# Grouped attention: a key's rotation, scalings and split spread over three heads

## The chip, the cores and the metric

The kernel runs on one core of a Trainium2 chip. The metric is the device time of one execution in microseconds (us), median of the runs. A core has engines that run side by side, each with its own instruction queue, and synchronise by semaphores: TensorE (PE, matrix products into PSUM; its weight loads are listed as PEld), VectorE (DVE), ScalarE (ACT), GpSimd (POOL) and SyncE (SP), which here issues the DMA transfers.

## The reference

A stack of two hybrid layers over x of shape (2, 512, 512), all in float32: narrow-head attention, two gated feed-forward blocks round a selective scan, grouped attention, a routed low-rank block, a top-k gated feed-forward block and the low-rank block again; each takes a layer-normalised x and is added to x. The change is in the grouped attention: 32 query heads of width 128 share 8 keys and values, four heads to a key.

```
q = q * cos + rotate_half(q) * sin          # the rotation, queries and keys
k = k * cos + rotate_half(k) * sin
scores = einsum('bhqd,bhkd->bhqk', q, k) / sqrt(128)
key_scale = where(kpos < 35, 0.5, where(kpos < 107, 1.5, 1.0))
scale = where(qpos >= 107, key_scale, 1)    # rows from 107 on only
probs = softmax(scores * scale + causal)
attn = einsum('bhqk,bhkd->bhqd', probs, v);  out = attn @ wo.T
```

## The kernel before, in words

The kernel writes each engine's program out by hand, in one order, with counted semaphores. A product of float32 matrices is made of three matmuls over operands that are split into a rounded high part and the difference as low part.

Grouped attention is the stage `gqa(b)`, run once for each batch b. Each engine has a function of that name; DVE's is at line 1542, PE's at 874, ACT's at 1179, and POOL's loop is at 573. All go through the heads h = 0 to 31 (GH = 32, G_REP = 4 heads to a key, G_KV = 8 keys). In the DVE and PE loops `part` is h % 4 and `g` is h // 4 - 1, the group of heads that has just been finished.

The work of a head is pipelined over several iterations. PE in iteration h makes the scores of head h + 1, turns the normalised probabilities of head h, projects the query of head h + 3 (into bank 7), makes the values product of head h, and in between one or two of the four output tiles of the group before: tiles 0 and 1 where part is 0, tile 2 where it is 1, tile 3 where it is 2. All four output tiles and the projected keys go through the one PSUM bank 3. PE waits there, by `claim(3, s["x_added"])`, until DVE has added the tile before into x. The next key but one is projected where part is 3.

A projected query or key becomes a rotated one as follows. DVE multiplies it by the cosines (`times_cos`, line 1546: `g_qc` for a query, `g_kc` for a key). ACT copies the two halves swapped into `g_sw` (two buffers, lines 1187 and 1188). POOL multiplies that by the sines (line 583), splits up to three weight units (lines 557 and 558), and for a query makes the low part (line 590), for which it needs the high part from DVE. DVE adds the two (`rope`, line 1551). For a query (`rope_q`) it then rounds the high part (line 1568). For a key (`rope_k`) it makes the high and low part of the first 128 columns (lines 1558, 1559), scales 35 columns by 0.5 and 72 by 1.5 (1560, 1561), and splits the whole key (1312, 1313 in the helper `split`); `g_k_split` tells PE that it may be used, which it does in the scores of head 4(g + 2), made in iteration 4(g + 2) - 1.

In DVE's iteration: the row maxima of the scores of head h + 1 (lines 1572 to 1602), a copy of a turned tile (1587), the low part of the values (1591), the rotation of the query of head h + 2, in heads 4, 8, ... 24 the rotation of a key, the cosine product of the query of head h + 3, two reciprocals of the row sums (1581), which ACT's normalising (line 1204) needs, and the adds into x (`add_rows`, line 1316).

Of the kernel before, what the change touches and what calls it, by code (L numbers as in the profile page):

```python
# [38 lines left out]
G_KV, G_REP, G_HD = 8, 4, 128  # L39
# [193 lines left out]
def hybrid_layers(nc, x_d, units_d, const_d, small_d, bdown_d, out_d):  # L233
# [9 lines left out]
    with ExitStack() as ctx:  # L243
# [3 lines left out]
        s = {n: ctx.enter_context(nc.semaphore(n)) for n in SEMS}  # L247
# [35 lines left out]
        def cut(stage, words, parts=1, dt=F32):  # L283

            at = cuts.get(stage, 0)
            cuts[stage] = at + words
            base, size = areas["rows" if stage in ("n", "l", "m_rows", "k_rows", "a_o") else "stages"]
            assert cuts[stage] <= size, (stage, cuts[stage])
            t = nc.alloc_sbuf_tensor_at(f"{stage}_{at}", [P, words * 4 // mybir.dt.size(dt)], dt, offset=base + 4 * at, align_bytes=4)
            return t[:, :] if parts == 1 else t[:, :].rearrange("p (a c) -> p a c", a=parts)  # L290
# [39 lines left out]
        g_sw, g_qk, g_kk = cut("g", 1024, 2), cut("g", 1024, 2), cut("g", 512)  # L330
# [3 lines left out]
        g_k_hi, g_k_lo = f_hi, f_lo  # L334
# [33 lines left out]
        def col(name, lo=0, hi=None):  # L368
            a, b = (CONST if name in CONST else SMALL)[name]
            t = const if name in CONST else small  # L370
            return t[:, a + lo:(a + hi if hi is not None else b)]
# [931 lines left out]
        def _(dve):  # L1303
# [6 lines left out]
            def split(hi, lo, src, sem):  # L1310

                did(V.tensor_copy(hi, src))
                did(V.tensor_tensor(lo, src, hi.bitcast(F32), ALU.subtract), sem)

            def add_rows(b, t, bank):
                go(V.tensor_tensor(x[:, b, t], x[:, b, t], ps[:, bank], ALU.add), s["x_added"])  # L1316
# [225 lines left out]
            def gqa(b):  # L1542
                dve.wait_ge(s["rope_in"], 16)
                def times_cos(out, bank, sem):
                    need(sem)
                    did(V.tensor_tensor(out, ps[:, bank], col("cos"), ALU.mult), s["g_cos"])

                def rope(out, part):

                    need(s["g_rot"])  # L1550
                    did(V.tensor_tensor(out, part, g_sw[:, done["swap"] % 2], ALU.add), s["g_roped"])  # L1551
                    done["swap"] += 1

                def rope_k(g):
                    rope(g_kk, g_kc)

                    k0, g = g_kk[:, 0:P], g % 2
                    did(V.tensor_copy(g_k0_hi[:, g], k0))  # L1558
                    did(V.tensor_tensor(g_k0_lo[:, g], k0, g_k0_hi[:, g].bitcast(F32), ALU.subtract))
                    go(V.tensor_scalar(g_kk[:, 0:SYS], g_kk[:, 0:SYS], 0.5, None, ALU.mult))  # L1560
                    did(V.tensor_scalar(g_kk[:, SYS:IMG], g_kk[:, SYS:IMG], 1.5, None, ALU.mult))
                    split(g_k_hi[:, g], g_k_lo[:, g], g_kk, s["g_k_split"])

                def rope_q(h):

                    reuse("g_qk", s["g_q_split"], 2)
                    rope(g_qk[:, h % 2], g_qc)
                    did(V.tensor_copy(g_q_hi[:, h % 2], g_qk[:, h % 2]), s["g_q_high"])

                def top(t, src=None):  # L1570
                    bank, at_s = g_bank[t]
                    return V.reduce_max(g_max[:, t:t + 1], ps[:, bank, at_s:at_s + (t + 1) * P] if src is None else src, AX.X)  # L1572

                def shifts(t):
                    pair = slice(t, t + 2)
                    did(V.tensor_scalar(g_sh[:, pair], g_max[:, pair], -G_HD ** -0.5, None, ALU.mult), s["g_shift"])

                def norms(t):

                    need(s["g_exp"], 2)  # L1580
                    go(V.reciprocal(g_inv[:, t:t + 2], g_sum[:, t:t + 2]), s["g_inv"])

                def keep_turned(h):
                    dve.wait_ge(s["g_turned"], (b * GH + h) * TT + 1)
                    if h or b:
                        dve.wait_ge(s["g_values"], b * GH + h)
                    go(V.tensor_copy(g_pT[:, 0:1, 0:P], ps[:, 4, 0:P].rearrange("p (a c) -> p a c", c=P)), s["g_pT_dve"])

                def values_low(h):
                    need(s["g_hi"])  # L1590
                    go(V.tensor_tensor(g_a_lo[:, h % G_KEEP], ps[:, 6], g_a_hi[:, h % G_KEEP].bitcast(F32), ALU.subtract), s["g_lo"])

                def add(t):
                    need(s["g_out"])
                    add_rows(b, t, 3)

                def maxima_1():

                    need(s["g_scores"])
                    go(top(1))  # L1600
                    did(V.tensor_tensor(g_s0, ps[:, 0, 0:P], col("key_scale"), ALU.mult))
                    did(V.tensor_tensor(g_s0, g_s0, col("mask"), ALU.add))  # L1602
                    did(top(0, g_s0))
                    shifts(0)

                def maxima_2():

                    need(s["g_scores"])
                    go(top(2))
                    need(s["g_scores"])  # L1610
                    did(top(3))
                    shifts(2)

                times_cos(g_kc, 3, s["g_k"])
                times_cos(g_qc, 7, s["g_q"])
                rope_k(0)
                rope_q(0)
                times_cos(g_kc, 3, s["g_k"])
                times_cos(g_qc, 7, s["g_q"])
                rope_k(1)  # L1620
                rope_q(1)
                maxima_1()
                maxima_2()
                times_cos(g_qc, 7, s["g_q"])
                norms(0)
                norms(2)
                for h in range(GH):
                    g, part = h // G_REP - 1, h % G_REP
                    if part == 1 and g >= 0:
                        add(1)  # L1630
                    if h + 1 < GH:
                        maxima_1()
                    keep_turned(h)
                    if h:
                        values_low(h - 1)
                    if h + 1 < GH:
                        maxima_2()
                    if part == 2 and g >= 0:
                        add(3)
                    if h + 2 < GH:  # L1640
                        rope_q(h + 2)
                    if part == 0 and h and g + 2 < G_KV:
                        rope_k(g + 2)
                    if h + 3 < GH:
                        times_cos(g_qc, 7, s["g_q"])
                    if h + 1 < GH:
                        norms(0)
                        norms(2)
                    if part < 2 and g >= 0:
                        add(2 * part)  # L1650
                    if part == 3 and g + 3 < G_KV:
                        times_cos(g_kc, 3, s["g_k"])
                values_low(GH - 1)
                for t in range(TT):
                    add(t)
# [20 lines left out]
            def topk(_):  # L1676
# [99 lines left out]
                for k in range(FK):  # L1776
                    low()
                add_accumulators(1, s["k_acc"])

            stages = dict(ln_rows=ln_rows, ln_turn=ln_turn, attn_qk=attn_qk, attn_heads=attn_heads, attn_out=attn_out, fmul=fmul, fdown=fdown, mproj=mproj, mssm=mssm,  # L1780
                          scan=scan, mback=mback, gqa=gqa, lora=lora, topk=topk)
            did(V.memset(eps[:, 0:1], LN_EPS), s["eps_set"])
            did(V.memset(eps[:, 1:2], RMS_EPS), s["eps_set"])
# [105 lines left out]
```

## Time and profile before

| | us |
|---|---|
| median of 3 runs | 3246.96 |
| lowest and highest run | 3235.99 and 3248.56 |
| the profiled execution's own time | 3246.35 |
| its span, first to last instruction | 3244.6 |
| PE busy | 2490.2 (77%) |
| DVE busy | 2017.2 (62%) |
| ACT busy | 1583.6 (49%) |
| POOL busy | 1121.2 (35%) |
| mean granted clock of PE | 0.863 of full |

The profile is of one execution. Busy time is a sum over the whole span. What a stage is bound by is seen in the rows of that stage: what an engine does, how long it was idle before an instruction, and which engine's instruction ended the idle time ("<-"). The granted clock is the mean, over a stretch, of what the chip allowed PE, as a share of full speed (2.4 GHz; the lower level is 1.2 GHz).

### The profile page before, as it was taken

Reading aid. Unit: us, or ns where it says so; the run is one execution under the profiler, and the core shown is the slowest. Engines: PE = TensorE matmul, PEld = TensorE weight load, DVE = VectorE, ACT = ScalarE, POOL = GpSimd, SP = SyncE. Lnnn points to the kernel's source line nnn. Section 1 sums busy time; section 2 is a strip of 40 time slices with the busy share of each in tenths; the row PEclk is TensorE's granted clock in tenths of the full one; section 3 lists DMA queues with packets and bytes.
Section 4 is the critical chain, followed back from the end, with each engine's and each line's share of the span. In section 5 each row is a group of like instructions: output and inputs, shape, how many; then the busy total and the mean of one; then the engine's idle time right before and its main releaser. Section 6 shows DMA issues by size and latency. Waiting matters only on the chain.

```text
span 3244.6 us, 36611 instructions
## 1 busy us (share of the span) xinstructions
PE 2490.2 (77%) x12408; PEld 1952.3 (60%) x12408; DVE 2017.2 (62%) x3083; ACT 1583.6 (49%) x3186; POOL 1121.2 (35%) x992
## 2 busy tenths in 40 slices
PE   6977989578678767678897989897989895951076
PEld 4334367467567656667786767676767674841065
DVE  4725635677676588777545666654666655298974
ACT  1532621466664176666212645552645551699611
POOL 2020055421223241122575454545454540210180
PEclk8797989689889878889998989998989897975587
DMA  6132222201100120100232011111111110100010
GB/s 205 41 119 62 54 69 62 65 20 35 38 20 30 33 72 14 53 20 23 62 95 65 30 49 30 56 43 56 33 46 37 52 40 14 39 26 0 0 46 26
DMA packets 85967, 152.56 MB, mean 47 GB/s; under 512 B 8632, under 2 KB 17464, under 8 KB 85656
## 3 DMA queue, kind: packets, MB, share of 16 engines
q1 hardware_dynamic: 85784, 150.24, 15.4%
q8 instruction: 101, 1.65, 0.2%
q14 instruction: 82, 0.67, 0.1%
HBM read 135.06 MB, written 14.75 MB: 46 GB/s over the span
## 4 chain that ended last, share of the span: by engine, by line
PE 33%; DVE 10%; ACT 8%; issue 4%; POOL 3%; POOLq 0%; DVEq 0%; ACTq 0%
PE ps L614 29%; ACT tables L1274 5%; PE ps L628 4%; DVE g L1551 1%; ACT m L1156 1%; POOL w_lo L558 1%; DVE g L1572 1%; ACT tables L1128 1%; POOL g L583 1%; DVE g L1558 1%; POOL k L571 1%; POOL g L590 1%; DVE stat L1328 1%; DVE x_sb L1316 0%; DVE g L1602 0%
## 5 line engine op out<-in xcount | busy, mean ns | idle before, releaser
L557 POOL TENSOR_SCALAR w_hi<-w_in 128x512 fp32r<-128x512 f32 x418 | 303.6, 726 | 1453.3 <-PE ps L614 895.3
L558 POOL TENSOR_TENSOR w_lo<-w_in,w_hi 128x512 fp32r<-128x512 f32 x418 | 605.1, 1448 | 34.8
L614 PE MATMUL ps<-hT_hi,w_lo 128*128 128x512 f32 x864 | 352.5, 408 | 17.4 <-DVE a L1358 11.1
L1517 DVE TENSOR_TENSOR_SCAN m<-m,m 128x1028 f32<-128x1028 f32 x128 | 307.6, 2403 | 67.6 <-ACT m L1156 60.2
L628 PE MATMUL ps<-tables,m 128*128 128x128 f32 x1024 | 186.5, 311 | 205.2 <-ACT tables L1128 120.4
L614 PE MATMUL ps<-hT_hi,w_hi 128*128 128x512 f32 x864 | 341.1, 395 | 0.0
L614 PE MATMUL ps<-hT_lo,w_hi 128*128 128x512 f32 x864 | 340.8, 394 | 0.0
L614 PE MATMUL ps<-m,tables 128*128 128x128 f32 (+1 forms) x2112 | 323.4, 302 | 12.7 <-ACT tables L1128 12.0
L614 PEld LDWEIGHTS ps<-m,tables 128*128 128x128 f32 (+1 forms) x2112 | 293.4, 213 | 22.6 <-ACT tables L1128 16.4
L628 PEld LDWEIGHTS ps<-tables,m 128*128 128x128 f32 x1024 | 128.6, 157 | 241.3 <-ACT tables L1128 144.0
L614 PE MATMUL ps<-w_hi,g 128*128 128x512 f32 x512 | 192.8, 439 | 84.0 <-DVE x_sb L1316 81.1
L1128 ACT ACTIVATE tables<-ps 128x512 f32<-128x512 f32 x256 | 150.7, 589 | 186.9 <-PE ps L628 183.4
L1156 ACT ACTIVATE m<-m_rows,negA 128x256 f32<-128x256 f32 x512 | 217.3, 498 | 0.4
L614 PE MATMUL ps<-g,g 128*128 128x128 f32 (+3 forms) x704 | 174.4, 397 | 37.6 <-POOL g L590 16.6
L614 PEld LDWEIGHTS ps<-hT_hi,w_lo 128*128 128x128 f32 x864 | 165.3, 191 | 54.2 <-DVE a L1358 14.5
L1316 DVE TENSOR_TENSOR x_sb<-x_sb,ps 128x512 f32<-128x512 f32 x120 | 82.0, 686 | 173.2 <-PE ps L614 172.9
L1211 ACT ACTIVATE g<-ps 128x256 f32<-128x256 f32 (+2 forms) x192 | 90.5, 491 | 200.3 <-PE ps L628 199.5
L614 PEld LDWEIGHTS ps<-hT_hi,w_hi 128*128 128x128 f32 x864 | 164.3, 190 | 37.2
L614 PEld LDWEIGHTS ps<-hT_lo,w_hi 128*128 128x128 f32 x864 | 165.1, 191 | 31.7
L614 PEld LDWEIGHTS ps<-g,g 128*128 128x128 f32 x704 | 123.4, 195 | 99.7 <-issue 62.5
L1389 DVE TENSOR_REDUCE a<-ps 128x2 f32<-128x1024 f32 x128 | 150.1, 1220 | 42.8 <-PE ps L614 42.3
L1078 ACT ACTIVATE a<-ps 128x512 f32<-128x512 f32 x256 | 138.9, 595 | 73.9 <-PE ps L614 73.4
(232 smaller groups left out, 5543.9 us busy)
## 6 DMA issues: line engine op xcount, KB each, us to landing
w_in<-units SPq DMA_DIRECT2D x418, 256.0 KB, 2.6
stack_scratch<-a SPq DMA_DIRECT2D x48, 256.0 KB
a<-stack_scratch SPq DMA_DIRECT2D x64, 192.0 KB, 4.4
m<-bc_scratch SPq DMA_DIRECT2D x16, 512.0 KB, 5.4
out<-x_sb SPq DMA_DIRECT2D x2, 1024.0 KB, 4.3
tables<-small SPq DMA_DIRECT2D x1, 1399.0 KB, 11.1
x_sb<-x SPq DMA_DIRECT2D x4, 256.0 KB, 3.5
x_sb<-x SPq DMA_DIRECT2D x1, 1024.0 KB, 8.3
```

Of the source, the lines that this page charges most:

```text
L557: c["did"](nc.gpsimd.tensor_scalar(w_hi[:, r], raw, 1.0, 1.0, ALU.mult, ALU.mult), s["unit_hi"])
L558: c["did"](nc.gpsimd.tensor_tensor(w_lo[:, r], raw, w_hi[:, r].bitcast(F32), ALU.subtract), s["unit_split"])
L614: ins = T.matmul(out, lhsT, rhs, start=start, stop=stop)
L628: ins = T.transpose(out, in_, ident)
L1078: go(A(a_pT[:, kT % 2 * 4 + pair * 2 + h], ps[:, 4 + h], ACT.Exp, scale=A_DK ** -0.5), s["a_exp"])
L1128: go(A(m_hT[:, part], ps[:, 6], ACT.Copy), s["m_hT_kept"])
L1156: go(A(m_dA[:, n % 2 * NG + r, 1:SEG], m_dt[:, i % 4], ACT.Exp, scale=negA[:, st:st + 1]), s["m_dA"])
L1211: go(A(g_pT[:, 0:t + 1, t * P:(t + 1) * P], ps[:, 4 + t % 2, 0:(t + 1) * P].rearrange("p (a c) -> p a c", c=P), ACT.Copy), s["g_pT_act"])
L1274: A(k_sign[:, done % 2], k_abs[b][t], ACT.Sign, bias=k_cand[:, b].bitcast(F32)[:, t:t + 1], scale=-1.0, accum_out=k_diff[:, b, t:t + 1]).t ...
L1316: go(V.tensor_tensor(x[:, b, t], x[:, b, t], ps[:, bank], ALU.add), s["x_added"])
L1389: go(V.reduce_max(top, ps[:, pair * 2:pair * 2 + 2], AX.X), s["a_max"])
L1517: V.tensor_tensor_scan(states, m_dA[:, dA:dA + NG].rearrange("p a t -> p (a t)"), states, 0.0, ALU.mult, ALU.add)\
```

## The change

The function `rope_k` on DVE is cut into three. What remains under the name is the rotation's add. `first_keys` has the two parts of the first 128 columns and the two scalings, `split_keys` the split. In the loop over heads the add stands behind the add of the first output tile (part 0), `first_keys` in the next head behind the rotation of the query (part 1), `split_keys` at the same place of the head after (part 2). The first two keys, ahead of the loop, are made in one piece as before (`whole_keys`). Nothing changes on the other engines.

```diff
-                def rope_k(g):
+                def rope_k():
                     rope(g_kk, g_kc)
+
+                def first_keys(g):
                     k0, g = g_kk[:, 0:P], g % 2
                     did(V.tensor_copy(g_k0_hi[:, g], k0))
                     did(V.tensor_tensor(g_k0_lo[:, g], k0, g_k0_hi[:, g].bitcast(F32), ALU.subtract))
                     go(V.tensor_scalar(g_kk[:, 0:SYS], g_kk[:, 0:SYS], 0.5, None, ALU.mult))
                     did(V.tensor_scalar(g_kk[:, SYS:IMG], g_kk[:, SYS:IMG], 1.5, None, ALU.mult))
-                    split(g_k_hi[:, g], g_k_lo[:, g], g_kk, s["g_k_split"])
+
+                def split_keys(g):
+                    split(g_k_hi[:, g % 2], g_k_lo[:, g % 2], g_kk, s["g_k_split"])
+
+                def whole_keys(g):
+                    rope_k()
+                    first_keys(g)
+                    split_keys(g)
...
                     if h + 2 < GH:
                         rope_q(h + 2)
-                    if part == 0 and h and g + 2 < G_KV:
-                        rope_k(g + 2)
+                    if part == 1 and 0 <= g < G_KV - 2:
+                        first_keys(g + 2)
+                    if part == 2 and 0 <= g < G_KV - 2:
+                        split_keys(g + 2)
                     if h + 3 < GH:
                         times_cos(g_qc, 7, s["g_q"])
                     if h + 1 < GH:
                         norms(0)
                         norms(2)
                     if part < 2 and g >= 0:
                         add(2 * part)
+                    if part == 0 and 0 <= g < G_KV - 2:
+                        rope_k()
                     if part == 3 and g + 3 < G_KV:
                         times_cos(g_kc, 3, s["g_k"])
```

## Rows read from the trace of the kernel before

**Rows 1.** PE's waits from head 4 to head 28: us in total, times, longest.

```profile
PE ps L614 <- DVE x_sb L1316: 38.1, 6, 7.0
```

**Rows 2.** Stretches of heads 4, 5, 8, 12, 16, 20, 24, 28; second batch, heads 4-28.

```profile
core 0: us, PE busy (x) PEld busy (x) DVE busy (x) ACT busy (x) POOL busy (x), PEclk, DMA share, GB/s
1816.19:1833.64 17.45, 14.03 (x70) 11.25 (x69) 10.83 (x25) 8.53 (x21) 8.80 (x8) 1.00 0.10 30
1833.64:1844.64 11.00, 11.00 (x58) 8.97 (x58) 6.32 (x16) 7.13 (x18) 2.59 (x3) 1.00 0.09 26
1866.70:1890.20 23.50, 16.53 (x70) 13.13 (x69) 14.42 (x24) 9.06 (x22) 15.38 (x15) 0.78 0.20 67
1923.30:1945.90 22.60, 15.63 (x70) 12.48 (x69) 14.43 (x25) 9.05 (x22) 15.38 (x15) 0.85 0.22 63
1978.97:2002.64 23.67, 16.70 (x70) 13.30 (x69) 14.43 (x25) 9.06 (x22) 15.38 (x15) 0.78 0.24 67
2035.70:2058.40 22.70, 15.73 (x70) 12.54 (x69) 14.42 (x24) 9.06 (x22) 15.38 (x15) 0.85 0.22 65
2091.50:2115.16 23.66, 16.82 (x70) 13.47 (x69) 14.29 (x25) 8.97 (x22) 15.88 (x16) 0.78 0.22 66
2147.05:2160.87 13.82, 13.82 (x70) 11.24 (x70) 8.54 (x17) 8.85 (x22) 12.81 (x13) 1.00 0.22 61
...
2297.44:2642.26 344.82, 305.37 (x1498) 247.09 (x1497) 217.40 (x448) 185.15 (x463) 181.23 (x167) 0.94 0.14 42
```

**Rows 3.** DVE in head 8, in order of time: start, length, engine, line.

```profile
1873.28 0.43 DVE L1568 CAST g<-g 128x512 fp32r<-128x512 f32 x1
1876.59 1.14 DVE L1551 TENSOR_TENSOR g<-loose,g 128x512 f32<-128x512 f32 x1 [2.88 <-POOL g L583]
...
1881.53 0.69 DVE L1313 TENSOR_TENSOR f_lo<-g,f_hi 128x512 fp32r<-128x512 f32 x1
...
1883.13 0.67 DVE L1316 TENSOR_TENSOR x_sb<-x_sb,ps 128x512 f32<-128x512 f32 x1
```

**Rows 4.** PE in head 8, its second output tile's first matmul.

```profile
1883.85 0.79 PE L614 MATMUL ps<-w_hi,g 128*128 128x512 f32 x1 [6.97 <-DVE x_sb L1316]
```

**Rows 5.** DVE in head 28, the adds of output tiles 0 and 1.

```profile
2155.15 0.69 DVE L1316 TENSOR_TENSOR x_sb<-x_sb,ps 128x512 f32<-128x512 f32 x1 [0.55 <-PE ps L614]
2160.12 0.69 DVE L1316 TENSOR_TENSOR x_sb<-x_sb,ps 128x512 f32<-128x512 f32 x1 [4.29 <-PE ps L614]
```

**Rows 6.** POOL in head 8, the key's product with the sines.

```profile
1875.22 1.27 POOL L583 TENSOR_TENSOR g<-g,tables 128x512 f32<-128x512 f32 x1
```

**Rows 7.** Head 5: DVE's cosine, ACT's swap and normalising, PE's next transposes.

```profile
1838.62 0.69 DVE L1546 TENSOR_TENSOR loose<-ps,tables 128x512 f32<-128x512 f32 x1
...
1840.79 0.60 ACT L1187 ACTIVATE g<-ps 64x512 f32<-64x512 f32 x1
...
1842.04 1.92 ACT L1204 ACTIVATE g<-g,g 128x128 f32<-128x128 f32 x4
...
1845.90 0.49 PE L628 MATMUL ps<-tables,g 128*128 128x128 f32 x3
```

**Rows 8.** DVE's lines of a key: count, shortest/median/longest ns, first and last start.

```profile
L1551 DVE TENSOR_TENSOR g<-loose,g x80: 684/695/1781, 1749.4 to 2646.1; 128x512 f32<-128x512 f32 x80
L1558 DVE CAST g<-g x16: 1168/1170/1200, 1750.6 to 2583.8; 128x128 fp32r<-128x128 f32 x16
L1559 DVE TENSOR_TENSOR g<-g,g x16: 293/727/1404, 1751.8 to 2585.0; 128x128 fp32r<-128x128 f32 x16
L1560 DVE TENSOR_SCALAR g<-g x16: 183/1210/1211, 1753.2 to 2585.8; 128x35 f32<-128x35 f32 x16
L1561 DVE TENSOR_SCALAR g<-g x16: 183/184/192, 1753.7 to 2586.9; 128x72 f32<-128x72 f32 x16
L1312 DVE CAST f_hi<-g x16: 426/428/1494, 1753.9 to 2587.1; 128x512 fp32r<-128x512 f32 x16
```

**Rows 9.** DVE in head 6, the query's cosine.

```profile
1852.81 0.69 DVE L1546 TENSOR_TENSOR loose<-ps,tables 128x512 f32<-128x512 f32 x1 [1.75 <-PE ps L614]
```

More of the change, by code:

```diff
@@ L1615, in gqa @@
                 times_cos(g_qc, 7, s["g_q"])
-                rope_k(0)
+                whole_keys(0)
                 rope_q(0)
@@ L1619, in gqa @@
                 times_cos(g_qc, 7, s["g_q"])
-                rope_k(1)
+                whole_keys(1)
                 rope_q(1)
```

## The prediction

> **What bounds the kernel now.** I read the busy shares first: no engine is full over the span, so the answer must come from the stage that the change touches. That stage is the grouped attention, which runs twice, once for each batch, 32 heads each. I cut it into heads at the maximum over 256 columns, the first thing that VectorE (DVE) does in a head. The table by stretches [rows 2] shows that an ordinary head takes 11.0 us, and TensorE (PE) is busy for all of them at a granted clock of 1.00: such a head is bound by PE. Heads 4, 8, 12, 16, 20 and 24, in which a key is rotated, take 17.45, 23.50, 22.60, 23.67, 22.70 and 23.66 us. Head 28 issues the same 70 matmuls, but no key is left to rotate; it takes 13.82 us with PE busy throughout. The list of waits names the difference: over heads 4 to 28 PE waited 38.1 us, in six waits, for the adds into x [rows 1], one in each head with a key.
>
> The timeline of head 8 shows the order. DVE stands still for 2.88 us until POOL has the key's rotated half [rows 3, 6]. Its add starts at 1876.59, then come two roundings, two scalings and the split, whose last instruction ends at 1882.22 (1881.53 + 0.69). Then the query's cosine, the reciprocals, and only at 1883.13 the add of the first output tile [rows 3]. PE has finished the head's values at about 1876.88 and may not write the second output tile into the one bank before that add: it idles 6.97 us, until 1883.85 [rows 4]. After that idling its clock is at the lower level (1.2 GHz) for a while: head 8 has a mean granted clock of 0.78, and its PE is busy 16.53 us with the matmuls that take 13.82 at 1.00 [rows 2]. After head 4's shorter stall (17.45 less 14.03, 3.42 us) it stays at 1.00.
>
> **The change part by part.** Nothing is added or dropped; the counts of instructions on every engine stay, and no wait on a new semaphore comes in. DMAs and SP's order are untouched, and POOL's and ScalarE's (ACT's) programs too. The key's eight DVE instructions move in three pieces.
>
> 1. *The rotation's add goes behind the add of the first output tile.* The query's cosine, both reciprocals and that add now follow the query's rounding directly. In head 8 the query's rounding ends at 1873.71 (1873.28 + 0.43 [rows 3]); the cosine (0.69 [rows 7]) brings 1874.4, the reciprocals 1874.7. PE's first output tile is then about done (head 28 has its add 8.10 us after its start, 2155.15 less 2147.05 [rows 2, 5]; by head 8's start of 1866.70 that is 1874.80). The add ends near 1875.5, 1.4 us before PE wants the bank: the stall of 6.97 us goes, and with it the slow clock. What is late next? The head then is PE's own work, as head 28 shows. The key's add follows: POOL's rotation ends at 1876.49 (1875.22 + 1.27 [rows 6]), and the add takes 1.14 [rows 3] (0.68 to 1.78 over all 80 of its shape [rows 8]), to 1877.7. DVE next needs the second output tile, which head 28 adds 13.07 us after its start (2160.12) after an idle 4.29 us [rows 5]; here 1879.8. So wait and add lie in DVE's idle time, with 2.1 us over. I cost the piece at nothing; without that cover it is at most 1.6 + 1.8 us a head.
>
> 2. *Roundings and scalings go into the next head.* They are one each of L1558 to L1561, 1.17 + 0.29 + 0.18 + 0.18 = 1.8 us at the least and 1.20 + 1.40 + 1.21 + 0.19 = 4.0 at the most [rows 8]. They stand ahead of a query's cosine and of the reciprocals, which ACT's swap and normalising wait for. In head 5 the cosine ends at 1839.31, ACT starts its swap at 1840.79 and its normalising at 1842.04; PE takes the first normalised tile at 1845.90 [rows 7]. With the cosine later by 1.8 to 4.0 us it ends at 1841.1 to 1843.3, the swap takes 1.25 (1842.04 less 1840.79) and one of the four normalisings 0.48 (1.92 / 4): 1842.8 to 1845.0. Both are ahead of 1845.90. I take nothing; what it would cost if more came on top is rival B.
>
> 3. *The split goes into the head after.* 0.43 to 1.49 for the rounding [rows 8] and 0.69 for the difference: 1.1 to 2.2 us, behind the query of head 6. There DVE waits 1.75 us for PE before the cosine at 1852.81 [rows 9], so 0 to 0.4 us come late, far inside the margin of piece 2. The scores that need the split key are PE's in head 7, 11 us later. Nothing.
>
> **POOL** does the same work in a shorter head: 15.38 us of it are in head 8 and don't fit in 13.8, so some 1.6 us spill into head 9, where POOL has little to do, as in head 5 (2.59 in 11.00 [rows 2]). In head 28 it is busy 12.81 of 13.82 and PE still has no gap [rows 2]. In issue order, the weight units that heads 9 to 11 need are split before the spilled ones. Nothing, but the spilled work meets DVE's instructions: rival B.
>
> A rule speaks against the change here. In rows 8 the same rounding of 128x128 never takes under 1.17 us, and the scaling of 35 columns takes 0.18 or 1.21; in head 8 the rounding runs while POOL splits a unit. The Trainium skill (SBUF — State Buffer, Who interferes with whom) says that VectorE and GpSimd share a pair of ports, and that for such casts and for operations with two SBUF inputs the one that starts second is blocked until the first ends. By that rule the moved pieces cost DVE up to their long form wherever POOL is at work; the trace agrees in the two lengths of one shape. It makes rival B what it is and changes nothing in the sum.
>
> **The sum.** First batch: 17.45 + 23.50 + 22.60 + 23.67 + 22.70 + 23.66 = 133.58 us for six heads, less 6 x 13.82 = 82.92: 50.7 us saved. Of these 38.1 are PE's waits [rows 1], and 12.6 the slow clock behind five of them. The second batch takes the same from head 4 to head 28 (344.82 us, against the 344.68 from 1816.19 to 2160.87 [rows 2]), so 50.8 more. Together 101.5 us. The profiled execution took 3246.35 us, 1.75 around its span of 3244.6; less 101.5 that is 3144.9. It lies 0.6 us under the median of the three runs (3246.96), which run from 3235.99 to 3248.56, so the scatter of a median is some 5 us. **3145 us.**
>
> **The rivals.**
> - *A, the forecast* (chance 0.80): all heads with a key become like head 28. Its own range is 3135 to 3156. For it: head 28, the same work without the key, in both batches. Against: that head has no next head with key work behind it.
> - *B, the stall partly comes back a head later* (0.14): the scalings, stretched by POOL's work and on top of stretched query operations (an add of 1.78 in place of 0.68, a rounding of 1.49 in place of 0.43 [rows 8]: 2.2 us), push the normalising to 1845.0 + 2.2 = 1847.2, 1.3 us after PE wants it; twelve times 1.3 is 16 us: 3161. With twice that lateness it is 3176. For it: POOL's spill. Against: the long forms never all fell together before (in head 8 these four and the split's rounding took 3.8 us together, from 1877.73 to 1881.53 [rows 3]).
> - *C, only half of it comes* (0.02): the waits go (38.1 + 38.3) and the clock is lower elsewhere in these heads all the same: 3246.4 - 76.4 = 3170. Against: head 5 and head 28 show 1.00 with PE full all through [rows 2].
> - *D, the other side: the key's add becomes the wait* (0.02). It now stands ahead of the next head's maxima. If POOL's rotation came late (behind weight splits), DVE would stand there, all softmax work of the next head with it. It costs nothing until the rotation's end is 2.1 us later than 1876.49 and PE feels it some 3 us after that; it eats the whole saving of 8.4 us a head (101.5 / 12) at about 13.5 us of lateness, and past that the kernel is slower. With 15 us: 1.5 x 12 = 18 us slower, 3264. Against: POOL takes the rotation straight after the query's low part, and nothing in POOL's order moves.
> - *E, it doesn't do what it says* (0.02): PE's second output tile waits for something that ends as late as DVE's add; then 3246. Against: the add ends at 1883.80 and PE starts at 1883.85.
>
> **How the numbers follow.** A is likeliest and gives the time. The range goes from 3130 (A with a median as low as the lowest of the runs before, 11 us under) to 3172 (C, and B to three quarters of its way). About 0.5% (16 us) is what a measurement of this kernel tells from no change. Faster by more: A, B and C, 0.96; within: E, 0.02; slower: D, 0.02.
>
> **What would show it.** Heads 4 to 24 at 13.8 us with a clock of 1.00 and no PE wait for the adds into x in them; the key's add behind the first output tile's, with a short wait for POOL or none, and the second tile's add still waiting for PE. Head 5's like still at 11.0. If these are at 12 with a PE wait for ACT's normalising, it is B; if the heads with a key are shorter but PE's clock still dips, C. A gain under 80 us or over 115 would make the prediction wrong.

## The result and the profile after

The changed kernel takes 3136.64 us (median of 4 runs, 3130.56 to 3150.28) where the kernel before takes 3242.07 (4 runs). The ratio is 0.9677, with a 95% interval from 0.9652 to 0.9702: 3.2% faster. Repeated as `e11_changed_again` beside another kernel it gave 0.9670 (0.9641 to 0.9698). The profiled execution took 3139.91 us, against 3246.35 before: 106.4 us less, where 101.5 were forecast. The median lies 8 us under the 3145 of the forecast, inside its range; some 5 us of that are the baseline, whose median was 3246.96 over three runs when the forecast was made and is 3242.07 over four.

The table by stretches of the changed kernel, columns as in [rows 2], for heads 4, 8, 9, 12, 16, 20 and 24 of the first batch and then heads 4 to 28 of both:

```profile
core 0: us, PE busy (x) PEld busy (x) DVE busy (x) ACT busy (x) POOL busy (x), PEclk, DMA share, GB/s
1816.15:1829.91 13.76, 13.76 (x70) 11.17 (x69) 8.66 (x18) 8.59 (x21) 8.87 (x8) 1.00 0.14 38
1863.01:1876.79 13.78, 13.78 (x70) 11.18 (x69) 9.27 (x18) 8.65 (x21) 11.81 (x11) 1.00 0.25 73
1876.79:1887.81 11.02, 11.02 (x58) 8.99 (x58) 8.76 (x22) 6.20 (x17) 6.02 (x6) 1.00 0.18 54
1909.87:1923.65 13.78, 13.78 (x70) 11.17 (x69) 9.46 (x18) 8.65 (x21) 11.78 (x12) 1.00 0.24 68
1956.72:1970.78 14.06, 14.06 (x72) 11.46 (x71) 9.16 (x18) 8.66 (x21) 12.02 (x12) 1.00 0.25 75
2003.59:2017.37 13.78, 13.78 (x70) 11.18 (x69) 9.24 (x18) 8.65 (x21) 11.84 (x11) 1.00 0.25 74
2050.45:2064.23 13.78, 13.78 (x70) 11.18 (x69) 9.62 (x18) 8.65 (x21) 11.78 (x12) 1.00 0.22 63
...
1816.15:2110.12 293.97, 292.69 (x1498) 238.19 (x1497) 212.46 (x448) 185.12 (x463) 183.91 (x167) 1.00 0.17 49
2246.06:2540.02 293.96, 292.69 (x1498) 238.18 (x1497) 211.41 (x448) 185.13 (x463) 183.75 (x167) 1.00 0.17 49
```

A head with a key went from between 17.45 and 23.67 us [rows 2] to 13.8, with PE busy all through at a clock of 1.00. (Head 16's stretch has 72 matmuls and 14.06 us, and the head behind it takes 10.75: the two together take 24.81, as head 8 and its successor take 24.80.) Heads 4 to 28 lost 50.7 us in the first batch (344.68 to 293.97) and 50.9 in the second (344.82 to 293.96): 101.6 together. The other 4.8 us of the profiled difference lie outside this stretch and are within the scatter between executions: outside heads 4 to 27 the profiles of the changed kernel and of `e1` to `e8` range from 2579.7 to 2607.1 us, and the changed kernel taken again has 2586.1.

PE's list of waits in the same stretch has nothing left of the line in [rows 1]:

```profile
PE ps L614 <- ACT g L1211: 0.7, 1, 0.7
PE ps L614 <- POOL g L590: 0.6, 1, 0.6
```

DVE in heads 8 and 9 of the changed kernel, in order of time as in [rows 3] (its lines have moved: L1577 is the query's rounding, L1560 to L1563 are the key's first parts and scalings):

```profile
1867.32 1.75 DVE L1551 TENSOR_TENSOR g<-loose,g 128x512 f32<-128x512 f32 x1
1869.10 0.43 DVE L1577 CAST g<-g 128x512 fp32r<-128x512 f32 x1
1869.57 0.69 DVE L1546 TENSOR_TENSOR loose<-ps,tables 128x512 f32<-128x512 f32 x1
...
1871.06 0.69 DVE L1316 TENSOR_TENSOR x_sb<-x_sb,ps 128x512 f32<-128x512 f32 x1 [0.54 <-PE ps L614]
1872.36 0.69 DVE L1551 TENSOR_TENSOR g<-loose,g 128x512 f32<-128x512 f32 x1 [0.61 <-POOL g L583]
1876.11 0.69 DVE L1316 TENSOR_TENSOR x_sb<-x_sb,ps 128x512 f32<-128x512 f32 x1 [3.05 <-PE ps L614]
...
1882.52 0.23 DVE L1560 CAST g<-g 128x128 fp32r<-128x128 f32 x1
1882.78 1.29 DVE L1561 TENSOR_TENSOR g<-g,g 128x128 fp32r<-128x128 f32 x1
1884.10 0.18 DVE L1562 TENSOR_SCALAR g<-g 128x35 f32<-128x35 f32 x1
```

The first tile's add now waits for PE, not PE for it. The key's add waits 0.61 us for POOL, in place of 2.88 in [rows 3], and is followed by 3.05 us of idleness: the cover that head 28 had promised with 4.29 [rows 5].

### The profile page after: what moved, and what is told of

The parts are those of the page before. It is cut to its first block, busy times and chain, and to the rows that moved or that the text cites. A ratio compares the mean times of both kernels' runs of the same rounds, so it can differ in the third digit from the quotient of the medians.

```text
span 3137.8 us, 36611 instructions
## 1 busy us (share of the span) xinstructions
PE 2461.8 (78%) x12408; PEld 1933.7 (62%) x12408; DVE 2008.0 (64%) x3083; ACT 1584.7 (51%) x3186; POOL 1127.0 (36%) x992
## 4 chain that ended last, share of the span: by engine, by line
PE 37%; ACT 8%; DVE 5%; issue 4%; POOL 3%; POOLq 0%; ACTq 0%; DVEq 0%
PE ps L614 33%; ACT tables L1274 5%; PE ps L628 4%; POOL w_lo L558 1%; ACT m L1156 1%; ACT tables L1128 1%; POOL w_hi L557 1%; POOL k L571 1%; DVE stat L1328 1%; DVE n L1336 0%; DVE tables L1748 0%; DVE f_lo L1313 0%; DVE x_sb L1316 0%; DVE f_hi L1312 0%; ACT m L1138 0%
## 5 line engine op out<-in xcount | busy, mean ns | idle before, releaser
L557 POOL TENSOR_SCALAR w_hi<-w_in 128x512 fp32r<-128x512 f32 x418 | 315.1, 754 | 1453.3 <-PE ps L614 886.9
L558 POOL TENSOR_TENSOR w_lo<-w_in,w_hi 128x512 fp32r<-128x512 f32 x418 | 596.5, 1427 | 34.9
L614 PE MATMUL ps<-hT_hi,w_lo 128*128 128x512 f32 x864 | 353.8, 409 | 19.2 <-DVE a L1358 12.9
L614 PE MATMUL ps<-m,tables 128*128 128x128 f32 (+1 forms) x2112 | 323.1, 302 | 13.3 <-ACT tables L1128 12.6
L614 PE MATMUL ps<-w_hi,g 128*128 128x512 f32 x512 | 177.0, 406 | 7.5 <-DVE x_sb L1316 4.7
```

Source lines behind the costliest of these rows:

```text
L557: c["did"](nc.gpsimd.tensor_scalar(w_hi[:, r], raw, 1.0, 1.0, ALU.mult, ALU.mult), s["unit_hi"])
L558: c["did"](nc.gpsimd.tensor_tensor(w_lo[:, r], raw, w_hi[:, r].bitcast(F32), ALU.subtract), s["unit_split"])
L614: ins = T.matmul(out, lhsT, rhs, start=start, stop=stop)
```

## The experiments

For each kernel I give the ratio to the kernel before, and from its profile the time from the start of head 4 to the start of head 28, both batches added. That second number is free of the scatter elsewhere: 661.8 us before, 560.2 in the changed kernel. The edits shown are against the changed kernel. `e5`, `e6` and `e7` rest on two runs each, the others on four or more.

| kernel | ratio (95%) | heads 4 to 27, us | over the changed kernel |
|---|---|---|---|
| changed | 0.9677 (0.9652 to 0.9702) | 560.2 | |
| `e1_rotation_back` | 0.9785 (0.9762 to 0.9808) | 593.9 | 33.7 |
| `e2_one_piece` | 0.9754 (0.9723 to 0.9785) | 573.1 | 12.9 |
| `e3_add_ahead` | 0.9817 (0.9785 to 0.9848) | 605.3 | 45.1 |
| `e5_linger_8` | 0.9893 (0.9856 to 0.9930) | 629.9 | 69.7 |
| `e6_linger_15` | 1.0124 (1.0035 to 1.0213) | 693.7 | 133.5 |
| `e7_next_head_4` | 0.9771 (0.9698 to 0.9844) | 573.4 | 13.2 |
| `e8_next_head_8` | 0.9906 (0.9877 to 0.9935) | 627.6 | 67.4 |

**One piece of the change undone: the key's add.**

```diff
+                    if part == 0 and 0 <= g < G_KV - 2:
+                        rope_k()
                     if part == 1 and 0 <= g < G_KV - 2:
                         first_keys(g + 2)
...
                         add(2 * part)
-                    if part == 0 and 0 <= g < G_KV - 2:
-                        rope_k()
```

> The changed kernel with the key's add (and DVE's wait for POOL) back ahead of the query's cosine and of the first output tile's add; the roundings and scalings stay in the next head and the split in the head after. Theory (the bank: what cost the time was the first tile's add coming late): in head 8 of the changed kernel POOL's rotation ends at 1872.3; the key's add then ends at 1873.5, the cosine at 1874.2, the reciprocals at 1874.4 and the first tile's add at 1875.2, while PE wants the bank 10.2 us after the head's start, at 1873.2. So 2.0 us of stall in heads 8 to 24 and some 0.4 in head 4, no fall of the clock: 2 x (5 x 2.0 + 0.4) = 21 us over the changed kernel, 3158. Rival (the spread: it was the amount of key work in one head that mattered, not what it stood in front of): with six of eight instructions gone from the head, within 5 us of the changed kernel, 3132 to 3142.

Measured: 3180.14 us where 3158 was expected, 33.7 us more in these heads where 21 were. The stalls are as worked out. PE before the second output tile of head 8 and of head 16:

```profile
1874.58 0.50 PE L614 MATMUL ps<-w_hi,g 128*128 128x512 f32 x1 [1.98 <-DVE x_sb L1316]
...
1973.03 0.50 PE L614 MATMUL ps<-w_hi,g 128*128 128x512 f32 x1 [2.00 <-DVE x_sb L1316]
```

and the stretches of the same two heads:

```profile
1862.42:1878.43 16.01, 14.03 (x70) 11.25 (x69) 9.59 (x18) 8.64 (x21) 13.81 (x14) 1.00 0.28 82
...
1960.85:1978.42 17.57, 15.57 (x70) 12.38 (x69) 9.61 (x19) 8.64 (x21) 14.98 (x14) 0.90 0.25 76
```

PE's waits for the add are 10.9 us in the first batch and 10.4 in the second, 21.3 in all. The rest of the 33.7 is the clock: I had expected none of it, but in heads 16, 20 and 24 of both batches it fell behind stalls of 2.0 to 2.3 us, and a head took 1.5 us more than head 8. The rival falls: with only the add and its wait for POOL in the old place, a third of the gain is gone.

**The whole key behind the first tile's add, not spread.**

```diff
-                    if part == 1 and 0 <= g < G_KV - 2:
-                        first_keys(g + 2)
-                    if part == 2 and 0 <= g < G_KV - 2:
-                        split_keys(g + 2)
...
                     if part == 0 and 0 <= g < G_KV - 2:
-                        rope_k()
+                        whole_keys(g + 2)
```

> All eight instructions of a key behind the first output tile's add, in one piece, in the same head. Theory (the bank): the key's work then ends 0.5 to 1.6 us after the second output tile is ready, so the next head's maxima are that much late, but PE takes the next normalised tile only some 4 us after ACT could have it there (the next head has no key work now): no time, 3137 within 5. Rival (the spread): DVE's whole key work in one head still delays what follows; at least half of the gain goes, 3185 or more.

Measured: 3169.13 us where 3137 within 5 was expected, and 12.9 us more in these heads; neither theory's number. By the ratios the kernel is some 25 us slower than the changed one (0.9754 less 0.9677), twice what these heads show. The profile is 27 us longer outside them, 22 of these before the stage begins; no run shows whether that belongs to the change or to the scatter. For the heads themselves my expectation missed twice. Behind the first tile's add the key's work meets POOL's weight splits, and DVE is busy with it to the end of the head. DVE in heads 8 and 9 of this kernel:

```profile
1896.23 0.53 DVE L1560 CAST g<-g 128x128 fp32r<-128x128 f32 x1
1896.80 1.41 DVE L1561 TENSOR_TENSOR g<-g,g 128x128 fp32r<-128x128 f32 x1
...
1898.93 1.49 DVE L1312 CAST f_hi<-g 128x512 fp32r<-128x512 f32 x1
1900.45 1.67 DVE L1313 TENSOR_TENSOR f_lo<-g,f_hi 128x512 fp32r<-128x512 f32 x1
1902.15 0.69 DVE L1316 TENSOR_TENSOR x_sb<-x_sb,ps 128x512 f32<-128x512 f32 x1
...
1904.68 0.29 DVE L1596 COPY g<-ps 128x128 f32<-128x128 f32 x1
```

Roundings and splits take 5.9 us here (1896.23 to 1902.12); the expectation's 1.6 us of lateness stood for 4.7 at most (3.05 of idle time and 1.6). And PE does not first meet the normalised tiles, but DVE's copy of the first turned tile (L1596), which frees bank 4:

```profile
1905.12 0.95 PE L628 MATMUL ps<-tables,g 128*128 128x128 f32 x7 [1.15 <-DVE g L1596]
```

Five such waits a batch, 5.6 us, make most of the 12.9. So by the profiles of these heads the place behind the add carries some 89 us of the 101.6, and the spreading the remaining 13.

**Only the first tile's add moved ahead.**

```diff
                     if h + 2 < GH:
                         rope_q(h + 2)
-                    if part == 1 and 0 <= g < G_KV - 2:
-                        first_keys(g + 2)
-                    if part == 2 and 0 <= g < G_KV - 2:
-                        split_keys(g + 2)
+                    if part == 0 and g >= 0:
+                        add(0)
+                    if part == 0 and 0 <= g < G_KV - 2:
+                        whole_keys(g + 2)
...
-                    if part < 2 and g >= 0:
-                        add(2 * part)
-                    if part == 0 and 0 <= g < G_KV - 2:
-                        rope_k()
+                    if part == 1 and g >= 0:
+                        add(2)
```

> The kernel before with one thing moved: the first output tile's add ahead of the key, which stays in one piece in front of the query's cosine and of the reciprocals. If PE waited for the bank alone, this gives the whole gain: 3137. By my theory there is a second release behind the key's work, ACT's swap and normalising: in head 8 the key ends at about 1877.9, the cosine at 1878.6, the reciprocals at 1878.8, ACT has the first normalised tile at 1880.3 and PE wants it at 1878.0. So a stall of some 2.3 us in heads 9, 13 and so on, less after head 4, with no fall of the clock: about 24 us over the changed kernel, 3160.

Measured: 3189.57 us where 3160 was expected, and 45.1 us more in these heads where 24 were. The wait for the add is gone and another has come in its place, as the theory says; PE in head 9:

```profile
1876.02 1.09 PE L628 MATMUL ps<-tables,g 128*128 128x128 f32 x3 [2.70 <-ACT g L1204]
```

It is 2.70 us where 2.3 were expected (13.4 and 13.5 us a batch), and the clock falls behind it (head 9 takes 12.40 us at a mean granted clock of 0.86), which the expectation left out. The bank was the first of two things that the key's work held up; the cosine and the reciprocals for ACT are the second.

**Pure lateness ahead of the first tile's add.** Idle maxima over the key's buffer, eight or fifteen, no work moved:

```diff
+                def linger(n):
+                    for _ in range(n):
+                        did(V.reduce_max(g_max[:, 0:1], g_kk, AX.X))
...
+                    if part == 0 and 0 <= g < G_KV - 2:
+                        linger(8)
                     if part < 2 and g >= 0:
                         add(2 * part)
```

> The changed kernel with eight idle row maxima over the key's buffer on DVE ahead of the first output tile's add in the six heads with a key: pure lateness, no work moved. In the changed kernel DVE is ready for that add at 1870.5 in head 8; eight at an estimated 0.6 us are 4.8 us, so the add ends at 1876.0 against 1873.2 when PE wants the bank. Theory (lateness of this one add is the whole price): a stall of 2.8 us in each of the twelve heads, 34 us, and where the clock falls behind it up to 1.7 us more (as behind the 2.0 us stalls of e1_rotation_back in three heads of five): 34 to 54 us over the changed kernel. Rival (the key's own work matters, by what it does to POOL and the split weights): a late add without it costs clearly less than 20 us.

> The same with fifteen: 9 us, the add ends at 1880.2 in head 8, 7.0 us after PE wants the bank, which is the stall that the kernel before had. Theory: the heads with a key take 23 to 24 us again with a clock near 0.8, and the time is that of the kernel before or slightly over, since head 4 now stalls in full too: 3240 to 3260. Rival: below 3220, because part of what the kernel before lost came from the key's work in its old place and not from the stall.

Both expectations were too low: 34 to 54 us over the changed kernel were expected with eight and 69.7 came (3215.29 us), and 3240 to 3260 us with fifteen, where 3290.38 came. One idle maximum took 0.69 us, not 0.6, so the eight took 5.7 us and the fifteen 10.8, and the stalls were 3.7 and 8.8 us in place of 2.8 and 7.0. PE's waits in heads 4 to 28 of the first batch, with eight:

```profile
PE ps L614 <- DVE x_sb L1316: 22.1, 6, 3.8
```

and with fifteen:

```profile
PE ps L614 <- DVE x_sb L1316: 52.4, 6, 8.8
```

With eight the cost is 69.7 us over twelve heads, 44 of it in waits; with fifteen 133.5, 105 in waits. The stall of the kernel before (6.97 us in head 8, 101.6 us of loss in all) lies between the two, and so does its price: waits of 22.1 and 52.4 us a batch go with 69.7 and 133.5, and the line between them gives 103.4 at the 38.1 of [rows 1]. So by this interpolation lateness alone, with no key work behind it, accounts for the loss. The rivals of both runs fall.

**How much room the moved pieces have.** The same idle maxima behind `first_keys`, four or eight (`linger(4)`, `linger(8)`):

> The changed kernel with four idle row maxima (an estimated 2.4 us) behind the roundings and scalings in heads 5, 9 and so on to 25: how much room the moved piece has left. In head 9 of the changed kernel ACT has the first normalised tile at 1886.9 and PE takes it at 1889.06, 2.2 us later. Theory: room of 2.2 us, so a stall of 0.2 us a head at most and 0 to 5 us in all. Rival B of the prediction in a harsher form (the room is already used up): 2 us a head, 24 us or more.

> The same with eight, 4.8 us. Theory: past the room of 2.2 us each further one costs twelve times: 2.6 x 12 = 31 us over the changed kernel, and some more if the clock falls behind these stalls. Rival (PE has other work to take meanwhile): under 10 us.

Four were 2.9 us late, for a room of 2.2, and PE's waits for ACT's normalising appear with 0.7 us each:

```profile
PE ps L628 <- ACT g L1204: 3.6, 5, 0.7
```

The cost is 13.2 us in these heads, where 0 to 5 were expected and 24 or more by the rival. Head 9 takes 12.18 us in place of 11.02. Part of what lies beyond the wait stands in the row of the wait itself: the three products on normalised tiles take 0.84 us together, where they take 0.49 without a wait.

```profile
1899.63 0.84 PE L628 MATMUL ps<-tables,g 128*128 128x128 f32 x3 [0.72 <-ACT g L1204]
```

Eight were 5.7 us late and cost 67.4 us, where 31 and some more for the clock were expected: 19.3 us of waits a batch and a lower clock behind them in the next head:

```profile
PE ps L628 <- ACT g L1204: 19.3, 6, 3.4
```

```profile
1918.49:1931.09 12.60, 11.56 (x50) 9.10 (x51) 9.41 (x20) 7.87 (x21) 3.05 (x3) 0.86 0.00 1
```

The room of 2.2 us is confirmed by the length of the waits (2.9 less 0.7, 5.7 less 3.4), and rival B's mechanism with it, though the changed kernel does not reach it. The price of a wait is not: by its length alone it came out too low in both runs.

**The same idea at the start, where PE still waits.** With the heads full, what is left of PE's idleness in the stage lies before head 0: in the changed kernel 8.6 us for POOL's low part of the first query and 6.8 for ACT's exponentials. `e9_start_too` interleaves the first two keys in the same way:

```diff
                 times_cos(g_kc, 3, s["g_k"])
                 times_cos(g_qc, 7, s["g_q"])
-                whole_keys(0)
-                rope_q(0)
+                rope_k()
                 times_cos(g_kc, 3, s["g_k"])
+                first_keys(0)
+                rope_q(0)
                 times_cos(g_qc, 7, s["g_q"])
-                whole_keys(1)
-                rope_q(1)
+                split_keys(0)
+                rope_k()
                 maxima_1()
+                rope_q(1)
                 maxima_2()
```

with `first_keys(1)` in head 0 and `split_keys(1)` in head 1.

> The changed kernel with the first two keys treated alike. Ahead of the loop: the second key's cosine right behind the first key's add, the first query's add before the first key's split, the second key's add before the first maxima and the second query's behind them; the second key's roundings and scalings go into head 0 and its split into head 1. PE idles 8.6 and 6.8 us there in each batch, for POOL's low part of the first query and for ACT's exponentials. Theory: DVE's order sets both waits; by moving about 2 us off the first and 5 off the second, and with less of the slow clock behind them, 5 to 8 us a batch are saved: 3125, between 3119 and 3129. Rival: POOL's weight splits and ACT's table load set them, and the time stays at 3137.

Measured: 0.9643 (0.9620 to 0.9666), median 3134.68, above the expected 3119 to 3129; by the runs the interval overlaps that of the changed kernel, so the gain is seen in the profiles only. From PE's first projection to head 4 the profile has 76.42 us in the changed kernel and 68.90 here:

```profile
1744.37:1813.27 68.90, 57.55 (x276) 46.37 (x277) 48.16 (x93) 39.07 (x95) 44.87 (x41) 0.93 0.17 47
```

and 5.7 us less in the second batch. The second wait went from 6.8 to 0.7 us, the first only from 8.6 to 7.9 (in the second batch from 8.6 to 9.5), now for the first key's split: behind it is POOL, which starts the first key's rotation after four weight splits of 2 us each.

Two kernels then changed POOL's order as well, `split_units(min(ready, at["u"] + early.get(name, 3)))` with a small table `early` for the first ropes:

```diff
-                    split_units(first_unit[n] + min(free["gk", 0] + RING - 1, len(names)))
+                    split_units(first_unit[n] + 6)
+                    early = {("gk", 0): 0, ("gq", 0): 0, ("gk", 1): 0, ("gq", 1): 1, ("gq", 2): 1,
+                             ("gq", 3): 2, ("gq", 4): 2, ("gq", 5): 2}
```

(`e12_start_pool_even`; `e10_start_pool` splits 5 ahead and has 0, 0, 2, 1 for the first four and 3 for the others.)

> e9_start_too with POOL's weight splits held back at the start of each batch's attention: it splits one unit ahead of the first rotation instead of four, none between the first two rotations, and catches up over the next ones. In the profile of e9_start_too PE idles 7.9 us before the first scores, for the first key's split, whose rotation POOL begins only behind four weight splits though ACT's swap is done some 4 us before. Theory: rotation and split come 4 to 7 us earlier, the stall falls to 1 to 3 us, and the clock doesn't fall behind it: 6 to 9 us a batch under e9_start_too, and 20 to 30 us under the changed kernel. Rival: the held-back weight units come late and PE waits for them: no gain over e9_start_too.

> e10_start_pool with the held-back weight splits spread evenly: six units ahead of the first rotation, none behind the first three, one behind each of the next two, two behind each of the following three. In e10_start_pool the first stall fell from 7.9 to 3.8 us, but POOL's two splits between the second key's and the second query's rotation put 2.6 us before the second scores, and three splits a head made heads 0 to 2 11.8, 10.5 and 9.8 us long. Theory: POOL's order sets all of these; the second scores come 4 us earlier and heads 0 to 2 fall back to 9.9, 9.2 and 9.2: some 8 us a batch under e10_start_pool, a ratio of 0.959 to 0.961 to the kernel before. Rival: ACT's table load and DVE's maxima set the start, and it stays at 0.964.

`e10_start_pool`: 3133.58 us, 0.9638 (0.9613 to 0.9663), no gain over `e9_start_too` clear of the noise, where 20 to 30 us under the changed kernel were expected. The first stall fell to 3.8 us, where 1 to 3 were expected, and heads 0 to 2 grew to 11.8, 10.5 and 9.8 us, since POOL's low parts of the queries came behind the splits made up for. It was the rival's outcome by another route: the units were in time, the queries were not. `e12_start_pool_even`: 3127.77 us, 0.9624 (0.9595 to 0.9653). Its start is 65.13 us in place of 76.42, with the second batch's shorter by 10.7:

```profile
1746.38:1811.51 65.13, 58.03 (x276) 46.18 (x277) 47.92 (x93) 38.98 (x95) 40.15 (x37) 0.95 0.15 41
```

That makes 22 us in the stage by the profile against the changed kernel, and 5.6 and 4.7 us a batch against `e10_start_pool`, where 8 were expected. By the runs it is the fastest kernel of the study and beats the kernel before by 3.8%, short of the ratio of 0.959 to 0.961 that was expected; over the changed kernel (0.9677 and 0.9670) its interval overlaps, so that step rests on the profiles.

## Why the prediction was right

- *What bounds the kernel.* Right: the heads with a key were PE's stalls on the bank of the output tiles, and what is left is PE's own work. Head 28 was the control that gave the number: 13.82 us predicted, 13.78 measured.
- *Piece 1, the key's add at no cost.* Right to a tenth. The first tile's add was put at the head's start + 8.10, and came at + 8.05 (1871.06 less 1863.01); the second tile's at + 13.07, and came at + 13.10. The wait for POOL stayed short because the rotation was done almost in time. In the bound beside it, "at most 1.6 + 1.8 us a head", the 1.6 doesn't follow from the forecast's own times, which give a wait of 1.0 (1876.49 less 1875.5); 0.61 came.
- *Piece 2, roundings and scalings at nothing.* Right: head 9 took 11.02 us as before. They took 1.86 us there (1882.52 to 1884.38), the low end of 1.8 to 4.0. That the sum met the low end is luck, since both of its large terms were wrong, one too high and one too low: a rounding that never took under 1.17 us before took 0.23, because in the new place it starts just ahead of POOL's instruction. The difference behind it, put at 0.29 for the low end, took a long form, 1.29. By the rule of the Trainium skill (SBUF — State Buffer, Who interferes with whom), the second to start is the one that is blocked; the trace agrees for the difference, which ends at 1884.07, right behind POOL's instruction (1882.63 to 1883.92). The room is now measured: 2.2 us.
- *Piece 3.* Right: heads 6, 10 and so on stayed at 11.0.
- *POOL.* Right in kind, wrong in size: 11.8 us of its work are left in head 8, and head 9 has 6.0 in place of 2.6. So 3.4 us spilled, not 1.6: the estimate let POOL work through all of head 8, and it is busy for 11.8 of its 13.8 us. It cost nothing, as forecast.
- *The sum.* 101.5 us predicted for these heads, 101.6 measured. Splitting it into 38.1 us of waits a batch and 12.6 of slow clock was right in size: in the second batch PE's busy time went from 305.37 to 292.69 us with the same 1498 matmuls, 12.7 less, and the time in which it was not busy from 39.5 to 1.3, 38.2 less. The runs with pure lateness agree with it.
- *The range.* It holds the result, but its lower end is not what its reason gives: 11 us under 3145 is 3134, not 3130. The measured 3136.64 is inside either.
- *The rivals.* B did not come, but e7 and e8 show it 2.2 us away. C and E fall with the profile. D did not come, and no run made POOL late to test it: POOL's rotation ended 0.6 us after DVE was ready for it, with 3.05 us of idle time behind. What the prediction did not see is a third release: in a bigger piece it would have been DVE's copy of the turned tile, not the normalising, that PE waits for first (e2).

## What to carry to other kernels

Where one engine's hand-written order makes another wait, look for what stands in front of the instruction that frees the buffer, and move what has a late due time behind it. Moving just the releasing instruction ahead won 56 of the 101.6 us (e3), since the work in between holds up the next release too; so list every release in the stretch with its own margin. A piece that occurs in some iterations and not in others gives the forecast for free: the iteration without it is the control.

## What the runs showed that was not expected

A stall of one length can cost two different sums, by whether the clock falls behind it. Each line is a head with the same matmuls, which take 13.78 us without a stall:

| kernel, head | PE's stall, us | head, us | mean clock | beyond 13.78 + stall |
|---|---|---|---|---|
| `e1_rotation_back`, 8 | 1.98 | 16.01 | 1.00 | 0.25 |
| `e1_rotation_back`, 16 | 2.00 | 17.57 | 0.90 | 1.79 |
| before, 4 | 3.42 | 17.45 | 1.00 | 0.25 |
| `e5_linger_8`, 4 | 3.50 | 19.09 | 0.91 | 1.81 |
| `e5_linger_8`, 12 | 3.73 | 20.44 | 0.83 | 2.93 |
| before, 12 | 6.97 | 22.60 | 0.85 | 1.85 |
| before, 8 | 6.97 | 23.50 | 0.78 | 2.75 |

A forecast that prices a short stall by its length alone can be out by up to 2.9 us for each, and the two expectations that did so (e1, e3) were too low by 13 and 21 us in these heads, 4 of the 21 by longer stalls. What decides whether the clock falls behind a stall of 2 us is open; it was not chance in the one run, since heads 16, 20 and 24 of `e1_rotation_back` fell in both batches and heads 8 and 12 in neither.
